# A decoder block in float32 halves: the q/k/v projection turned so that weights stay and tokens move, rotation once per unit, batches two at a time

## What is computed

```
x = x + attention(layernorm(x))      # 32 heads of 64, 8 key/value heads, causal, rotary embedding
x = x + cross(layernorm(x), ctx)     # both rounded to fp8 by blocks of 128, then einsum emk,enk->emn
x = x + moe(layernorm(x))            # 8 experts of hidden size 704, top 1, capacity 256, plus a shared expert

xq = (x @ wq), xk = (x @ wk), xv = (x @ wv)            # per batch
xq = xq * cos + rotate_half(xq) * sin ; xk likewise    # 64 wide, halves of 32 swapped
out = softmax(mask(xq xk' / 8)) xv ; out @ wo
```

## Time and profile before

| | |
|---|---|
| median of 3 runs | 1687.62 us (1686.0 to 1688.01) |
| profiled execution, its own time | 1689.58 us |
| its span | 1687.8 us |
| mean granted clock of TensorE | 0.963 |

### The profile page before, as it was taken

The page is one execution under the profiler, slowest core; times in us unless marked ns, Lnnn a source line. Parts: engine busy times, 40 slices in busy tenths (PEclk is TensorE's granted clock), DMA queues, the critical chain, the costliest instruction groups (busy, mean ns, idle before and its releaser), DMA issues.

```text
span 1687.8 us, 28887 instructions
## 1 busy us (share of the span) xinstructions
PE 1527.2 (90%) x9640; PEld 1409.0 (83%) x9640; DVE 1340.3 (79%) x3545; ACT 997.0 (59%) x2741; POOL 849.2 (50%) x945
## 2 busy tenths in 40 slices
PE   4789999999999999999999996674797979799997
PEld 4679999999999999999999995564696968799996
DVE  7688888888888888888888887985888875577785
ACT  2577777777777777777777775423121213465662
POOL 1345555565565565465465456644525351455455
PEclk9899999999999999999999998896898989899998
DMA  4000000000000000000000031012010101677766
GB/s 145 1 20 13 1 20 14 2 20 14 1 20 13 2 20 14 1 20 14 2 20 13 8 125 57 19 62 90 32 44 32 32 26 38 189 218 233 226 211 226
DMA packets 46355, 95.20 MB, mean 56 GB/s; under 512 B 5382, under 2 KB 5894, under 8 KB 46208
## 3 DMA queue, kind: packets, MB, share of 16 engines
q1 hardware_dynamic: 43648, 85.10, 15.5%
q0 software_dynamic: 2560, 8.25, 1.5%
HBM read 76.70 MB, written 16.78 MB: 55 GB/s over the span
## 4 chain that ended last, share of the span: by engine, by line
PE 70%; DVE 15%; ACT 6%; issue 6%; POOL 1%; DMA 1%; another core or an unknown queue 1%; DVEq 0%; SPq 0%; POOLq 0%; ACTq 0%
PE bank L365 14%; PE bank L366 14%; PE bank L367 14%; PE bank L411 6%; PE bank L395 4%; PE bank L426 4%; PE bank L427 4%; PE bank L383 4%; PE bank L382 4%; ACT P L683 2%; PE bank L357 2%; DVE P L954 1%; DVE work L1014 1%; DVE PTl L985 1%; DVE work L900 1%
## 5 line engine op out<-in xcount | busy, mean ns | idle before, releaser
L1328 POOL TENSOR_TENSOR P<-P,ri 128x128 f32<-128x128 f32 (+3 forms) x512 | 355.1, 726 | 202.7 <-DVE ri L943 195.7
L683 ACT ACTIVATE P<-P,mn 128x512 f32<-128x512 f32 (+3 forms) x512 | 286.7, 560 | 219.1 <-DVE mn L954 218.6
L954 DVE CUSTOM_DVE_ANT_0 P<-bank,mask 128x512 f32<-128x512 f32 (+3 forms) x512 | 235.9, 479 | 41.4 <-PE bank L383 41.4
L985 DVE TENSOR_TENSOR PTl<-bank,PTh 128x512 fp32r<-128x512 f32 (+1 forms) x384 | 230.9, 602 | 36.2 <-ACT PTh L703 30.1
L365 PE MATMUL bank<-XT,Uh 128*128 128x256 f32 x704 | 204.3, 290 | 18.3 <-ACT XT L726 10.0
L411 PE MATMUL bank<-ident,P 128*128 128x128 f32 x1280 | 204.6, 275 | 0.0
L703 ACT ACTIVATE PTh<-bank 128x512 fp32r<-128x512 f32 (+1 forms) x384 | 200.8, 524 | 6.3 <-PE bank L411 3.4
L367 PE MATMUL bank<-XT,Ul 128*128 128x256 f32 x704 | 201.8, 287 | 0.0
L366 PE MATMUL bank<-XT,Uh 128*128 128x256 f32 x704 | 201.7, 287 | 0.0
L1342 POOL TENSOR_TENSOR OTl<-Opair,OTh 128x512 fp32r<-128x512 f32 x64 | 82.9, 1295 | 226.6 <-ACT OTh L720 226.5
L382 PE MATMUL bank<-KT,QT 128*128 128x256 f32 (+2 forms) x512 | 187.7, 367 | 8.6 <-DVE mn L954 8.6
(11 more groups left out here) (167 smaller groups left out, 3975.2 us busy)
## 6 DMA issues: line engine op xcount, KB each, us to landing
RW<-in_wf SPq DMA_DIRECT2D x170, 256.0 KB, 3.0
work<-in_ctx SPq DMA_DIRECT2D x32, 256.0 KB, 2.7
Wraw<-in_wqkv SPq DMA_DIRECT2D x8, 768.0 KB, 4.4
Wraw<-in_wo SPq DMA_DIRECT2D x8, 512.0 KB, 3.5
xd<-work SPq DMA_DIRECT2D x16, 256.0 KB, 3.3
XN<-xd SPq DMA_DIRECT2D x8, 512.0 KB, 5.0
oe<-work SPq DMA_DIRECT2D x16, 256.0 KB, 2.2
out<-X SPq DMA_DIRECT2D x16, 256.0 KB
```

Source lines behind the costliest of these rows:

```text
L683: e.activation(pq, pq, ACT.Exp, bias=mn[:, z, qb:qb + 1], scale=-1.0, accum_out=rs[:, z, qb:qb + 1]).then_inc(a_exp, 1)
L954: e.tensor_tensor_reduce(P[:, z, off[qb]:off[qb] + k], bank[n % 2][:, 0:k], mask[:, 512 - k:512], -0.125, BIG, ALU.add, ALU.min, mn[:, z, ...
L985: e.tensor_tensor(pt_part(PTl, part), bank[2 + part][:, 0:128 * n].rearrange("p (m n) -> p m n", n=128), pt_part(PTh, part).bitcast(F32), ...
L1328: e.tensor_tensor(pq, pq, ri[:, z, qb:qb + 1].to_broadcast([128, n]), ALU.mult).then_inc(g_norm, 1)
```

## The change

The projection is turned: 128 weight columns are stationary and the 512 tokens of a whole batch move, so q and k come out feature by token and need no turn. A unit's 36 matmuls are three groups of twelve, in the steps k = 0, 1 and 2 of the unit's four (k is h modulo 4): first halves of the four q heads, second halves, then k and v. Step k = 3 has none. Only v is turned back (`turn_v`, 4 transposes of 64 rows, in step k = 0 of the next unit). Unit u is projected in steps 4u-8 to 4u-6 and its q, k and v are made ready in steps 4u-4 to 4u-2.

Rotation is done once for a unit: DVE multiplies both q halves by cos and sin (four products of 128x512 out of PSUM, in steps k = 1 and 2, each step's first product ahead of `masked` block 1 and its second behind `pt_lo` part 0), POOL adds and subtracts them (`rotate`, k = 2), ACT rounds the result (`query_hi`, k = 0 of the next unit), POOL takes the low half (`query_lo`, 128x1024, k = 1), and 16 DMAs place the heads in QT. k's halves are swapped by two DMAs, and POOL multiplies, adds and takes the low half (64x512 each); one DMA doubles the result over the partitions.

Batches go two at a time: XT has two buffers instead of four, a pair of units shares one group's weights, so weights are loaded and split 15 more times after the first instead of 7 (every 8 steps), now in three parts for Wqkv and with a buffer of its own for Wo, whose split lies in step k = 3 of every second unit (h = 8ep + 7), the step whose `attn_out` is the first to use it. Batches 2 and 3 are normed and turned in steps 52 to 59 through bank 5. Names and buffers of the cross block move (YT1, T1, T2), its order does not.

```diff
-            def project(n):
-                u, i = divmod(n, 4)
-                g, b = divmod(u, NB)
-                ps = bank[proj_bank(n)][:, 0:384]
...
-                    last = three(ps, xh, xl, Wh[:, c, :], Wl[:, c, :], c == 0, c == 3)
-                last.then_inc(p_proj, 1)
+            def project(u, part, c):
+
+                ps = bank[7 if part == 1 else 6][:, :]
+                cols = slice(128 * part, 128 * part + 128)
...
+                last = three(ps, Wh[:, c, cols], Wl[:, c, cols], T[:, 0, c, :], T[:, 1, c, :], c == 0, c == 3)
...
-                if 0 <= h + 6 < NH:
-                    project(h + 6)
+                if unit < NU and k < 3:
+                    for c in range(4):
+                        project(unit, k, c)
```

On DVE (`rotate` and its place; `unit, k = divmod(h + 8, 4)`):

```diff
+            def rotate(u, second, fn):
+
+                T = q2s if second else qcs
+                need.wait_ge(p_q, 2 * u + 1 + second)
+                need.wait_ge(d_tab, 48)
+                if second:
+                    need.wait_ge(g_rot, u)
+                else:
+                    need.wait_ge(a_qh, u)
+                    need.wait_ge(g_ql, u)
+                last = e.tensor_tensor(T[:, fn, :], bank[7 if second else 6][:, :], rope[:, fn, :], ALU.mult)
...
-                if 0 <= h + 5 < NH:
-                    rotate(h + 5)
+                if after_unit and k == 0:
+                    key_cos(unit - 1)
+                if after_unit and k == 1:
+                    value_lo(unit - 1)
+                if unit < NU and k in (1, 2):
+                    rotate(unit, k - 1, 0)
...
+                if unit < NU and k in (1, 2):
+                    rotate(unit, k - 1, 1)
+                if h >= 0 and h % 8 == 0 and 0 < h // 8 + 1 < NEP:
+                    split_wq_lo(h // 8 + 1)
...
-                if 0 <= h + 5 < NH:
-                    parts_qk(h + 5)
+                if h >= 15 and h % 8 == 7 and h // 8 < NEP:
+                    split_wo_lo(h // 8)
                 if 0 <= h - 7 < NH:
                     attn_out(h - 7)
```

On POOL:

```diff
+            def query_lo(u):
+                need.wait_ge(a_qh, u + 1)
+                if u:
+                    wait_q(need, u - 1)
+                e.tensor_tensor(ql[:, :, :], qcs[:, :, :], qh[:, :, :].bitcast(F32), ALU.subtract).then_inc(g_ql, 1)
...
+                for part, at in ((0, -10), (2, -7)):
+                    ep, rest = divmod(h - at, 8)
+                    if rest == 0 and 0 < ep < NEP:
+                        split_wq_lo(ep, part)
                 if 0 <= h - 1 < NH:
                     normalised(h - 1)
-                if 0 <= h + 5 < NH:
-                    rotate(h + 5)
+                if h >= 15 and h % 8 == 7 and h // 8 < NEP:
+                    split_wo_lo(h // 8)
+                if after_unit and k == 0:
+                    rotate_key(unit - 1)
+                if after_unit and k == 1:
+                    query_lo(unit - 1)
+                if after_unit and k == 2:
+                    key_lo(unit - 1)
...
                 if 0 <= h - 3 < NH:
                     pair(h - 3)
+                if unit < NU and k == 2:
+                    rotate(unit)
```

More of the change, by code:

```diff
@@ L13 @@
 NP, UP, NR = 17, 11, 6
+NEP = NU // 2
 CHUNK_BANK = (4, 5, 7)
@@ L87, in decoder @@
         X = sb("X", [128, NT, D])
-        XT = {b: sb(f"XT{b}", [128, 2, 4, 512], F32R) for b in (0, 2, 3)}
+        XT = [sb(f"XT{b}", [128, 2, 4, 512], F32R) for b in range(2)]
         ident = sb("ident", [128, 128])
@@ L599, in ffn @@
                         e.matmul(ps, Hh[:, 5, sl], Dl[:, 5, :], start=False, stop=True).then_inc(p_down, 1)
-            def late_first_turn(h):
-                if TB <= h + 8 < NT:
-                    wait_bank5(need, h, "first_turn")
-                    first_turn(h + 8, 5)
             for t in range(TB):
                 first_turn(t, t)
-            for h in range(-6, NH + 7):
+            for h in range(-8, NH + 7):
+                unit, k = divmod(h + 8, 4)
                 if 0 <= h < NH:
@@ L623, in tensor_engine @@
                     turn_p(h - 2, 1)
-                if 0 <= h + 4 < NH:
-                    turn_qk(h + 4, True)
+                if 0 < unit <= NU and k == 0:
+                    turn_v(unit - 1)
                 if 0 <= h < NH:
@@ L668, in next_wo, with split_wq @@
-            def next_wo(g, half):
-                need.wait_ge(p_ao, 16 * g)
-                split_w(Oraw, Oh, half, 2 * g + 2)
-            def value_hi(n):
-                u, i = divmod(n, 4)
-                need.wait_ge(p_proj, n + 1)
+                if b >= 2:
+                    need.wait_ge(p_kv, 13 + b)
+                e.activation(XT[b % 2][:, 0, :, tokens(i)], four(bank[k][:, :]), ACT.Copy).then_inc(a_xt, 1)
+            def split_wq(ep, part):
+                cols = slice(128 * part, 128 * part + 128)
+                need.wait_ge(d_wq, 16 * (ep + 1))
+                if part == 2:
+                    need.wait_ge(p_kv, 2 * ep)
+                elif ep:
+                    need.wait_ge(p_q, 4 * ep - 1 + part)
+                e.activation(Wh[:, :, cols], Wraw[:, :, cols], ACT.Copy).then_inc(a_wq, 1)
@@ new lines, in split_wo, with values_keys, value_hi @@
+            def split_wo(ep, half):
+                need.wait_ge(d_wo, 16 * (ep + 1))
+                need.wait_ge(p_ao, 8 * ep)
+                e.activation(Oh[:, half, :], Oraw[:, half, :], ACT.Copy).then_inc(a_wo, 1)
+            def values_keys(u):
+                need.wait_ge(p_kv, u + 1)
+                need.wait_ge(p_vt, u)
+                need.wait_ge(d_kr, 32 * u)
+                e.activation(kvs[:, :], bank[6][:, :], ACT.Copy).then_inc(a_kv, 1)
+            def value_hi(u):
+                need.wait_ge(p_vt, u + 1)
@@ L679, in exp, with query_hi @@
+            def query_hi(u):
+                need.wait_ge(g_rot, u + 1)
+                if u:
+                    wait_q(need, u - 1)
+                e.activation(qh[:, :, :], qcs[:, :, :], ACT.Copy).then_inc(a_qh, 1)
             def exp(h, qb):
@@ L1239, in vector_engine @@
                 first_turn(t, t)
+            split_wq_lo(0)
             for t in range(TB, 2 * TB):
                 first_stats(t)
+            rstd_of(slice(TB, 2 * TB))
+            for t in range(TB, 2 * TB):
+                first_norm(t)
             pieces = list(range(NP))
-            for h in range(-6, NH + 7):
+            for h in range(-8, NH + 7):
+                unit, k = divmod(h + 8, 4)
+                after_unit = 0 < unit <= NU
                 if h == 0:
-                    need.wait_ge(a_w, 4)
-                    split_w_lo(Oraw, Oh, Ol)
-                gq, nq = divmod(h + 6, 16)
-                go, no = divmod(h - 7, 16)
+                    split_wo_lo(0)
                 if 0 <= h - 1 < NH:
```

541 lines of the change are left out of this document (288 added, 253 removed).

## The result

The changed kernel takes 1851.94 us (median of 4 runs, 1850.79 to 1852.88) beside 1687.82 us for the kernel before: a ratio of 1.0967, 95% interval [1.0946, 1.0988], 164 us slower. I had forecast slower, 1772, with a range up to 1825: the direction and the two waits were right, the change that I forecast was half of the measured one.

The account below looks back on a forecast made before the run. The prediction took PE to bound the kernel, with other engines close behind. On 1689.6 us its terms, -70 - 14 + 85 + 6 + 53 + 9 - 6 + 20 = +83, gave about 1772 us, range 1705 to 1825.

Parts of the forecast that it names:

- the 20 us for the clock: PE's clock drops to 0.50 behind idle times in steps with a Wo split: +20 us taken, between 0 and 42.
- the rival in which these matmuls wait for their weights: PE's projection saving is lost as 512-column matmuls wait for weight loads: near 1790 us, called unlikely, no separate chance.
- The k = 1 wait: DVE's first product waits for POOL's query_lo, delaying PE's attn_out and next weigh: +85 us over 30 steps.
- The upper bound of 126: Upper bound for DVE waiting on query_lo in k = 1: 30 x 4.2 us.
- The k = 3 wait: PE's attn_out waits for the Wo split on DVE and POOL: +53 us over 14 steps, bounds 45 and 60.
- the term of -70 us: PE saves 2.2 us a unit through wider projection matmuls and fewer turns: -70 us for 32 units if PE stayed the bound.
- First turns: Turns of batches 2 and 3 now lie in full steps, so weigh starts later: +1.7 us x 8 = +14.
- The first scores: Start of the first scores, at 50.82 us before: about as early, 0 change, within 5 us either way.
- The splits of before: PE idle time caused by the old Wqkv and Wo weight splits goes away: -14 us, bounds 7 and 17.
- The last steps: Final steps, where the cross block loads DVE, lose three steps' rotations: -6 us.
- Covered waits (faster): query_lo and the Wo split finish before they hold anything up: 1615 us, up to 1675 with a few waits; chance 0.12.
- The clock rival: The clock falls behind both kinds of wait: about 1835 us; chance 0.14 for clock or both waits longer, over 1805.

Follow-up runs that it names:

- the fill: Changed kernel plus 20 matmuls with unused output on PE in each of 12 steps with a Wo split, before attn_out: 1818.1 us, ratio 1.0784.
- both waits moved: Changed kernel with query_lo first in POOL's k = 1 list and the Wo split at the head of its k = 3 step: 1708.4 us, ratio 1.0118.
- the control: Kernel before the change with only turn_p part 0 put ahead of weigh on PE: 1687.2 us beside 1690.1, ratio 0.9987.
- the move: Changed kernel with query_lo first, Wo split at the head of its step, and turn_p part 0 ahead of weigh on PE: 1693.5 us, ratio 1.0029.
- runs of nine: Changed kernel with nine projection matmuls per step: 1685.2 us; also Wo split at the head: 1664.1; also turn_p ahead of weigh and DVE's products adjacent: 1607.9.

## Why the prediction was right in direction and half in size

**Where the missing 80 us lie.** By the forecast's terms eight steps take 67.9 us and, with a fifteenth of the 20 us for the clock, 69.3. They took 75.1. Step by step, without the clock, the forecast has 8.9 us for k = 3 with a Wo split (11.9 measured), 8.15 for k = 0 (9.3 and 8.9), 11.5 and 10.0 for the two kinds of k = 1 (12.4 and 9.5), 7.87 for k = 2 (8.2 and 8.9) and 5.5 for the plain k = 3 (5.95). The largest single gap is the 3.0 us of the step with the Wo split, about 42 us in 14 of them. The rest lies mostly in k = 0 and k = 2, which had no wait in the forecast.

**PE's own work: right in sum.** The projection costs 0.228 us for a matmul of 512 columns in all kernels, so the rival in which these matmuls wait for their weights is out. A unit without waits takes 29.05 us where 29.0 were worked out (8.15 + 7.87 + 7.87 + 5.13). That the two agree so closely is partly luck: the four turns of v cost 0.55 us (7.68 against 7.12), where I took 0.3 with 0.36 as the upper bound, and each step is otherwise some 0.06 shorter than worked out. The work is saved; the changed kernel doesn't collect it.

**The k = 1 wait: right in place and cause, close in size.** DVE waits for g_ql behind POOL's multiplications; 97 us came back when it was moved, 85 forecast. The upper bound of 126 prices the plain units at 4.2 us too; by the terms given it is 95. The Wqkv split's k = 1 step is 12.4 us against 11.5 worked out, and 10.6 where the fill keeps the clock up; the plain one is 9.5 against 10.0, and hands 0.8 us on to its k = 2 step, where weigh waits for DVE.

**The k = 3 wait: right in cause, too small. This is the first step that failed.** The term was +53 us, from a step of 8.9 us; the step takes 11.9. Of the 3.0 us, 1.8 are POOL's queue: attn_out starts at T+9.2 instead of T+7.4. T+6.9 to 7.4 for POOL's half comes out with pair at T-0.9. The earlier trace rows and the earlier trace rows, of a k = 1 step, have ACT's piece at T-0.8 and POOL's at T-0.06, and at a k = 3 step POOL's piece stands at T+0.97, in the kernel before already. So rotate, the multiplications and the split were all later, and the split took 1.70 us instead of 1.29. The other 1.2 us are the low clock: the filled step takes 10.7. Moving the split gives 50 us back.

**The covers that went, missed. This is the second.** The prediction took the 24 turns off as work, in the term of -70 us, and asked what stood behind the added waits, but not what the removed turns covered. weigh waited for nothing before because 0.36 us of turns stood ahead of it. The run with both waits moved has steps of 8.9, 8.1, 8.1 and 5.95 us, 31.0 for a unit where I had 29.0 + 0.4: 1.6 us a unit, 48 us in 30 units. The 0.22 over 7.87 in each of k = 1 and k = 2 are this cover: these steps fell from 8.09 to 7.81 when turn_p took the place, and the control gained next to nothing. In k = 0, 0.7 us are over: weigh starts 0.43 later than T+0.80, behind the same addition, and 0.25 are the dearer turns of v. The plain k = 3 step holds 0.8 us (0.4 forecast), and there the move gave nothing, as PE waits for join. The move gave 15 us in all with twelve matmuls in three steps; with nine in every step each of k = 0 and k = 1 gained 0.3 us.

**The clock: right in kind, 20 us taken.** The fill experiment gave 34 us back, within the bounds of 0 and 42 of that term, 14 above what I took. Those bounds counted only the steps with a Wo split; by the lengths of the steps 1.2 of 3.0 us lie in the k = 1 and k = 2 steps. The low clock stood behind the idle times of 5.1 us in each step with a Wo split from 9 to 116, outside the first turns, and behind the 2.8 to 2.9 us in k = 1.

**The rest.** First turns cost +13.4 us, forecast +14. The first scores came at 48.8 us, forecast 50.8 within 5, and steps 0 to 8 are 7 us shorter, forecast 5. The splits of before had cost 2.0 us in sixteen steps (64.45 and 62.45 us for the eight with them and without), as worked out. The last steps gave nothing, forecast -6; behind step 116 the kernel is 2 us longer. q and k landed in time: apart from the very first scores, ahead of which PE waits 2.3 us for a DMA of KT, no idle time of PE in k = 0 is ended by their DMAs.

**The rivals.** Covered waits (faster) is wrong as the kernel stands, and its number, 1615, is close to what the lists can give once waits and covers are put right (1607.9). The clock rival, at 1835 (its own terms add up to 1839), was nearest to the measured time, but for the wrong reason: it counted 87 us for the clock, and the fill gave 34 back.

## What to carry to other kernels

When work leaves the engine that sets the pace, look at what it stood in front of: a short piece of work between two others may be all that hides a wait, and it appears then in every step that has nothing longer to wait for. In a pipeline of ordered lists, spread the work of a unit evenly over its steps: with the long waits out of the way, 12, 12, 12 and 0 matmuls cost 31.0 us for a plain unit and nine in each 30.8, no great matter; but the steps with a Wo split took 8.0 to 9.2 us in the one and 7.41 in the other, and covering the short waits brought a unit to 30.8 in the one and 29.05 in the other. In whole kernels even groups gave 44 us (1708 to 1664) and, with the covers, 86 (1693 to 1608). The runs of nine also use each projection a step later, so the share of the spreading itself isn't separated from that. Before an instruction is given a wait on a slower engine, add up that engine's whole list ahead of the result, pieces of the step before included and read from a step of the same kind, and put the consumer a step later if it doesn't fit.

## What was not expected of the hardware

Adding 240 matmuls that compute nothing made the kernel 34 us faster, by keeping the granted clock of TensorE at 1.00 where it was 0.50, the lower level of 1.2 GHz, behind idle times of 5.1 us. Shorter idle times gave both outcomes. Behind 2.8 to 2.9 us in k = 1 the clock was low each time. With both waits moved it was low behind 9 of 12 idle times of 2.4 us ahead of attn_out, and in the filled kernel behind 4 of 13 of 2.2 to 2.3 us. No run here shows what decides in a single case.
